# Second mixture-of-experts FFN: one shared-expert block moved behind the expert tiles, with its weights' loads, bias adds and combines rearranged

## The reference, cut to what matters

```
x = x + 0.5 * ffn(layernorm(x));  x = x + attn(layernorm(x));  x = x + 0.5 * ffn(layernorm(x))

ffn(x):                                   # 4096 tokens, D = 256
  weights, idx = gate(x)                  # 2 of 16 experts per token
  h  = silu(x @ We1[e] + be1[e]) * (x @ We3[e] + be3[e])     # 128 wide
  y  = sum over the 2 chosen of weight * (h @ We2[e] + be2[e])
  z  = silu(x @ ws1 + bs1) * (x @ ws3 + bs3) @ ws2 + bs2     # shared, 256 wide
  return y + z
```

## Time and profile before

| | |
|---|---|
| median of 3 runs | 1149.94 us (1148.79 to 1150.99) |
| profiled execution | 1148.11 us, its span 1146.4 us |
| busy share of the span | TensorE 90%, ScalarE 76%, VectorE 67%, GpSimd 40% |
| head (routing, four shared blocks) | about 877 to 929.5 |
| turns | 929.5 to 1093.5 |
| tail (four shared blocks, 16 combines, output) | 1093.5 to 1146.4 |

### The profile page before, as it was taken

How to read it: one execution, slowest core, us unless ns; L and a number is a source line. 1 busy time by engine, 2 the same in 40 slices (tenths; PEclk the granted TensorE clock), 3 DMA queues, 4 the chain that set the end, 5 groups by cost and what they waited for, 6 DMA issues and landing times.

```text
span 1146.4 us, 23653 instructions
## 1 busy us (share of the span) xinstructions
PE 1028.5 (90%) x7546; PEld 558.4 (49%) x7549; DVE 772.9 (67%) x1565; ACT 871.3 (76%) x1251; POOL 461.9 (40%) x671
## 2 busy tenths in 40 slices
PE   8998999989787787989889998989899988999996
PEld 4456999946554122222122222322224568998854
DVE  6898788768996514544255547467768678678866
ACT  4326777746887999999999999999997236777710
POOL 1003666467730424421222223431413345677755
PEclk8999999999999899999999999999999999999998
DMA  8911555445766121020201022120101944566554
GB/s 288 276 57 51 172 166 169 151 132 174 226 195 207 48 71 56 10 62 10 65 10 54 18 70 79 33 71 19 48 1 38 308 147 150 163 188 180 175 177 152
DMA packets 125717, 133.79 MB, mean 117 GB/s; under 512 B 13224, under 2 KB 111888, under 8 KB 125616
## 3 DMA queue, kind: packets, MB, share of 16 engines
q1 hardware_dynamic: 109056, 90.95, 25.0%
q0 software_dynamic: 14448, 39.47, 12.4%
q10 hardware_dynamic: 2112, 2.10, 0.5%
HBM read 80.43 MB, written 52.04 MB: 116 GB/s over the span
## 4 chain that ended last, share of the span: by engine, by line
PE 26%; ACT 26%; issue 15%; DVE 10%; DVEq 1%; POOL 1%; DMA 1%; ACTq 0%; POOLq 0%
ACT wide L2073 23%; PE banks L2445 6%; PE banks L1957 5%; PE banks L2370 4%; PE banks L2457 3%; PE banks L2379 2%; PE banks L1931 2%; DVE x_res L1628 1%; PE banks L2433 1%; PE banks L1453 1%; DVE wide L1677 1%; DVEq L2653 1%; PE banks L1456 1%; PE banks L1971 1%; DVE attn_lines_parts L190 1%
## 5 line engine op out<-in xcount | busy, mean ns | idle before, releaser
L2073 ACT ACTIVATE wide<-banks 128x1536 f32<-128x1536 f32 (+1 forms) x384 | 492.3, 1491 | 4.2 <-PE banks L1931 3.3
L1957 PE MATMUL banks<-wide,attn_attend_v_now 128*32 128x512 f32 (+3 forms) x2560 | 288.7, 542 | 2.4 <-POOL wide L2083 2.4
L2083 POOL TENSOR_SCALAR_AFFINE_SELECT wide<-wide 128x256 f32<-128x256 f32 (+1 forms) x320 | 116.3, 394 | 387.7 <-ACT wide L2073 385.3
L1931 PE MATMUL banks<-attn_attend_q_now,attn_attend_k_now 32*128 32x512 f16 (+3 forms) x1280 | 150.7, 355 | 56.9 <-ACT wide L2073 53.8
L1931 PEld LDWEIGHTS banks<-attn_attend_q_now,attn_attend_k_now 32*128 32x128 f16 x1280 | 38.7, 91 | 292.5 <-ACT wide L2073 248.3
L668 POOL DMA_INDIRECT f_region<-xn_rows,f_token_of x79 | 78.9, 999 | 124.7 <-DVE f_token_of L899 82.7
L2128 DVE COPY sums<-banks 128x512 f32<-128x512 f32 x32 | 22.1, 691 | 134.3 <-PE banks L1957 134.1
L2445 PE MATMUL banks<-f_xnt 128*128 128x128 f32 x752 | 101.4, 278 | 10.1 <-DVE f_more L2671 7.2
L2133 DVE RECIPROCAL below<-below 128x512 f32<-128x512 f32 x32 | 107.3, 3353 | 1.1
L2445 PEld LDWEIGHTS banks<-f_xnt 128*128 128x128 f32 x752 | 91.3, 191 | 15.1 <-ACT f_xnt L2523 8.8
L2553 POOL DMA_INDIRECT last_rows_in<-xn_rows,f_spare x72 | 70.2, 975 | 66.9 <-DVE f_stage L2614 23.6
(11 more groups left out here) (368 smaller groups left out, 1811.5 us busy)
## 6 DMA issues: line engine op xcount, KB each, us to landing
y_half<-f_xnt SPq DMA_DIRECT2D x94, 128.0 KB
y_slots<-wide SPq DMA_DIRECT2D x79, 128.0 KB, 1.7
attn_v<-f_more SPq DMA_DIRECT2D x32, 256.0 KB
attn_attend_v_now<-attn_v SPq DMA_DIRECT2D x32, 256.0 KB, 3.1
x_res<-L_attn_x SPq DMA_DIRECT2D x8, 512.0 KB, 7.4
xn_rows<-f_w_all SPq DMA_DIRECT2D x8, 512.0 KB, 5.4
attn_q<-attn_lines_q_out SPq DMA_DIRECT2D x8, 512.0 KB, 3.4
attn_k<-attn_lines_k_out SPq DMA_DIRECT2D x8, 512.0 KB, 3.9
```

Of the source, the lines that this page charges most:

```text
L1931: last = pe.matmul(score[i % SLOTS][:, j, column:column + columns(u)], k_now[rows, kt * P:(kt + 1) * P], q_now[rows, qc * QW + c0:(qc + 1) ...
L1957: last = pe.matmul(out_bank[qc][rows, c0:QW], v_now[:, kt, rows], probs[:, place, column:column + columns(u)], start=(kt == 0), stop=(u == ...
L2073: act.activation(probs_flat[:, at:at + width_of[i]], score_flat[i % SLOTS][:, 0:width_of[i]], ACT.Exp, scale=SCALE).then_inc(sem.exp_done, 1)
L2083: pool.affine_select(out=part, in_=part, compare_op=ALU.is_ge, fill=0.0, base=0, pattern=[[0, part.shape[1]], [1, P]], channel_multiplier= ...
```

## The change

- `SHARED_FIRST` goes from 4 to 3: block 3 of the shared expert is computed in the tail, with five blocks there. In the head VectorE's `offset` comes before `add_shared(2)`.
- The rings that lay in the space of `xnt` lie in blocks 0 to 2 of it alone; `y_rows` goes to `s.lin`, the fourth place of `w_up` to a tensor of its own.
- SP issues the loads of We2 and be2 (2 MB each) before it waits for the stores; We1 and We3 stay behind.
- GpSimd adds `bs2` to the second half's blocks, after `bring(11)` and before it waits for `prod_ready`; VectorE's four adds are gone.
- Ten combines lie between turns in place of 16. The rows of tiles 10 to 15 are fetched into places of the row ring whose last turn is over (`left_row`), and combined in the tail.
- The tail's order on VectorE is new: combines in groups, and `add_shared(i)` after the combines of block i (`finish`), where it came before them. SP waits for `z_added` as well. The last two parts of the output are one of two tiles.

```diff
-SHARED_FIRST = 4
+SHARED_FIRST = 3
...
+    w_two, gated = ring(2, UP, 0), ring(2, P, 0)
+    rows_t, w_one = ring(2, D, 1), ring(1, UP, 1)
+    w_up = [w_two[:, 0, :], w_two[:, 1, :], w_one[:, 0, :], w_fourth[:]]
+    y_rows = s.lin[:].rearrange("p f n -> p (f n)").rearrange("p (n w) -> p n w", n=ROUND)
...
+    row_left = {place: n for n in range(TURNS) for place in (row_place(n),)}
+    left_rows = sorted((n, place) for place, n in row_left.items() if place < ROWS - ROWS // 4 or place >= ROWS)
+    def left_row(t, k):
+        return left_rows[TOPK * (t - BACK_LATE) + k]
     def back(t, k):
-        return back_first[:, 2 * (t % BACK_FIRST) + k, :] if t < HT else back_second[:, 2 * (t - HT) + k, :]
+        if t >= HT:
+            return back_second[:, 2 * (t - HT) + k, :]
+        if t >= BACK_LATE:
+            return rows_in(left_row(t, k)[0])
+        return back_first[:, 2 * (t % BACK_FIRST) + k, :]
...
     def sync(sp):
         sp.wait_ge(before.exp_done, ends.exps)
         sp.wait_ge(before.pv_done, ends.values)
+        sp.dma_start(w_all[:, :, UP:UP + D], w["We2"]...)
+        sp.dma_start(w_all[:, :, UP + D:], over_partitions(w["be2"], P, E, D))...
         for q in range(2):
             sp.wait_ge(s.stored[q], 16 * (BLOCKS - 2) // 2)
...
-        sp.dma_start(w_all[:, :, UP:UP + D], w["We2"]...)
-        sp.dma_start(w_all[:, :, UP + D:], over_partitions(w["be2"], P, E, D))...
...
             sp.wait_ge(sem.combined, end_tile)
+            sp.wait_ge(sem.z_added, end_tile // 2)
...
         shared_down(1)
-        shared_up(3, (0, 1))
         pe.wait_ge(first.pairs_ready, 2)
         routing.count(pe, bank[7])
-        shared_up(3, (2, 3))
         shared_down(2)
-        shared_down(3)
...
-            if k == 0 and BACK_FIRST <= t < HT:
+            if k == 0 and BACK_FIRST <= t < BACK_LATE:
                 pool.wait_ge(sem.combined, t - BACK_FIRST + 1)
+            elif BACK_LATE <= t < HT:
+                pool.wait_ge(sem.combined, t - BACK_RING + 1)
+                pool.wait_ge(sem.rows_turned, left_row(t, k)[0] + 1)
...
         for n in range(4, 12):
             bring(n)
+        pool.wait_ge(first.staged, BLOCKS)
+        for b in range(HB, BLOCKS):
+            part = x[:, b * BT:(b + 1) * BT, :]
+            pool.tensor_tensor(part, part, s.bs2..., ALU.add).then_inc(first.bs2_added, 1)
         pool.wait_ge(sem.prod_ready, SHARED_FIRST)
...
         routing.keep_counts(dve, 1, bank[7])
-        multiply(3)
+        routing.offset(dve, 1)
         add_shared(2)
-        routing.offset(dve, 1)
-        add_shared(3)
...
-        for b in range(HB, BLOCKS):
-            part = x[:, b * BT:(b + 1) * BT, :]
-            dve.tensor_tensor(part, part, s.bs2..., ALU.add).then_inc(first.bs2_added, 1)
+        def finish(i):
+            dve.wait_ge(sem.combined, (i + 1) * BT)
+            add_shared(i)
         dve.wait_ge(first.bs2_added, BLOCKS)
-        (multiply 4, 5; add 4; combine 16..18; multiply 6; combine 19; add 5; ...)
+        combine_some(BACK_LATE, HT - 1)
+        multiply(3)
+        combine_some(HT - 1, HT + 2)
+        multiply(4)
+        combine_some(HT + 2, HT + 3)
+        finish(3)
+        combine_some(HT + 3, HT + 6)
+        multiply(5)
+        finish(4)
+        combine_some(HT + 6, HT + 10)
+        multiply(6)
+        finish(5)
+        combine_some(HT + 10, HT + 14)
+        multiply(7)
+        finish(6)
+        combine_some(HT + 14, HT + 16)
+        finish(7)
...
-OUT_PARTS = [... (TILES - 4, TILES - 2), (TILES - 2, TILES - 1), (TILES - 1, TILES)]
+OUT_PARTS = [... (TILES - 4, TILES - 2), (TILES - 2, TILES)]
-COMBINE_AT = (61, 64, 67, 70, 73, 76, 79, 82, 84, 85, 87, 88, 90, 92, 93, 95)
+COMBINE_AT = (61, 64, 67, 70, 73, 76, 79, 82, 85, 88)
+BACK_LATE = len(COMBINE_AT)
```

More of the change, by code:

```diff
@@ L2282, in ffn_by_halves @@
     bs = sb("bs", [P, 2 * SHARED // P])
+    w_fourth = sb("w_fourth", [P, UP])
     ws13, ws2, prod_t, bias_rows = s.ws13, s.ws2, s.prod_t, s.bias_rows
@@ L2289, in ffn_by_halves, with ring @@
     back_second = w_all[:].rearrange("p e f -> p (e f)")[:, 0:HT * TOPK * D].rearrange("p (n d) -> p n d", d=D)
[L2290 to L2297, removed]
+    taken = [0, 0]
+    def ring(n, width, c):
+        at = taken[c]
+        taken[c] += n * width
+        assert taken[c] <= SHARED_FIRST * BW
+        return s.xnt[:, c, at:at + n * width].rearrange("p (n w) -> p n w", n=n)
+    w_two, gated = ring(2, UP, 0), ring(2, P, 0)
+    rows_t, w_one = ring(2, D, 1), ring(1, UP, 1)
+    w_up = [w_two[:, 0, :], w_two[:, 1, :], w_one[:, 0, :], w_fourth[:]]
+    y_rows = s.lin[:].rearrange("p f n -> p (f n)").rearrange("p (n w) -> p n w", n=ROUND)
     sem = semaphores(nc, tag, "experts_loaded bias_turned bias_ready xnt_ready "
@@ L2334, in sync @@
         sp.wait_ge(before.pv_done, ends.values)
+        sp.dma_start(w_all[:, :, UP:UP + D], w["We2"].rearrange("e i d -> i e d")).then_inc(sem.experts_loaded, 16)
+        sp.dma_start(w_all[:, :, UP + D:], over_partitions(w["be2"], P, E, D)).then_inc(sem.experts_loaded, 16)
         for q in range(2):
@@ L2341, in sync @@
                          ).then_inc(sem.experts_loaded, 16)
-        sp.dma_start(w_all[:, :, UP:UP + D], w["We2"].rearrange("e i d -> i e d")).then_inc(sem.experts_loaded, 16)
-        sp.dma_start(w_all[:, :, UP + D:], over_partitions(w["be2"], P, E, D)).then_inc(sem.experts_loaded, 16)
         for n in range(TURNS):
@@ L2444, in up @@
                     col_at = (2 * c + f) * INTER
-                    last = pe.matmul(bank[2 + m][:, f * P:(f + 1) * P], w_up[:, at, col_at:col_at + INTER],
+                    last = pe.matmul(bank[2 + m][:, f * P:(f + 1) * P], w_up[at][:, col_at:col_at + INTER],
                                      rows_t[:, m, c * P:(c + 1) * P], start=(c == 0), stop=(c == DC - 1))
@@ L2573, in gpsimd @@
             bring(n)
+        pool.wait_ge(first.staged, BLOCKS)
+        for b in range(HB, BLOCKS):
+            part = x[:, b * BT:(b + 1) * BT, :]
+            pool.tensor_tensor(part, part, s.bs2.rearrange("p (o d) -> p o d", o=1).to_broadcast([P, BT, D]), ALU.add).then_inc(first.bs2_added, 1)
         pool.wait_ge(sem.prod_ready, SHARED_FIRST)
@@ L2670, in multiply_rows @@
                 dve.wait_ge(sem.y_done, n - ROUND + 1)
-            dve.scalar_tensor_tensor(prod_t[:, at, :], bank[2 + n % 2][:, P:2 * P], w_up[:, at, UP - 1:UP], gated[:, n % 2, :], ALU.add, ALU.mult
+            dve.scalar_tensor_tensor(prod_t[:, at, :], bank[2 + n % 2][:, P:2 * P], w_up[at][:, UP - 1:UP], gated[:, n % 2, :], ALU.add, ALU.mult
                                      ).then_inc(sem.prod_done, 1)
@@ L2675, in combine @@
             dve.wait_ge(fetch_of(t), fetches(t))
[L2676 removed]
+            if t < SHARED_FIRST * BT:
+                dve.wait_ge(sem.z_added, 2 * (t // BT) + t % BT // 2 + 1)
             dve.scalar_tensor_tensor(tile(t), back(t, 0), core.weight[:, 0, t:t + 1], tile(t), ALU.mult, ALU.add).then_inc(sem.first_added, 1)
@@ L2709, in vector, with combine_some @@
                 combine(combine_at[n])
-        for b in range(HB, BLOCKS):
-            part = x[:, b * BT:(b + 1) * BT, :]
-            dve.tensor_tensor(part, part, s.bs2.rearrange("p (o d) -> p o d", o=1).to_broadcast([P, BT, D]), ALU.add).then_inc(first.bs2_added, 1)
-        dve.wait_ge(first.bs2_added, BLOCKS)
[L2714 to L2731, removed]
+        def combine_some(first_tile, end_tile):
+            for t in range(first_tile, end_tile):
+                combine(t)
+        def finish(i):
+            dve.wait_ge(sem.combined, (i + 1) * BT)
+            add_shared(i)
+        dve.wait_ge(first.bs2_added, BLOCKS)
+        combine_some(BACK_LATE, HT - 1)
[15 more added lines that the diff above has]
+        finish(7)
     return Programs(sync, tensor, scalar, gpsimd, vector, (sem, row_loaded, row_stored))
 INVERT_AT, BACK_FIRST, BACK_RING = 26, 4, 2 * BT
-OUT_PARTS = [(t, t + 4) for t in range(0, TILES - 4, 4)] + [(TILES - 4, TILES - 2), (TILES - 2, TILES - 1), (TILES - 1, TILES)]
+OUT_PARTS = [(t, t + 4) for t in range(0, TILES - 4, 4)] + [(TILES - 4, TILES - 2), (TILES - 2, TILES)]
 BACK_TURN = HALF_TURNS + ROWS + LENT + 6
-COMBINE_AT = (61, 64, 67, 70, 73, 76, 79, 82, 84, 85, 87, 88, 90, 92, 93, 95)
+COMBINE_AT = (61, 64, 67, 70, 73, 76, 79, 82, 85, 88)
+BACK_LATE = len(COMBINE_AT)
 FFN_NAMES = "gate_w gate_b We1 be1 We2 be2 We3 be3 ws1 bs1 ws2 bs2 ws3 bs3"
```

4 lines of the change are left out of this document (2 added, 2 removed).

## The result

The changed kernel takes 1154.88 us (median of 5, 1152.8 to 1157.8) against 1150.23 us for the kernel before, measured beside it: ratio 1.0042, 95% interval 1.0029 to 1.0056. It is slower by 4.7 us. The forecast was slower by 2.3 us, 1152.2, with a range up to 1154.8: the measured time lies just outside. The side and the kind of the likeliest case were right; its size was half of what came. In the profiled executions the span went from 1146.4 to 1151.1 us.

A forecast was written before the change was run, and what follows sets the result against it. VectorE was taken to bound the start, its combines the turns' end, the fetches the tail. Start +1.9, turns' end -4.0 and tail +4.4 gave +2.3 us, thus 1152.2 us, range 1145.3 to 1154.8.

The forecast's parts named there:

- the likeliest case: Port held: GpSimd's bias adds keep VectorE's two-SBUF-input operations waiting in the head; 1150.3 to 1154 us, chance 0.60.
- What bounds the start: Start of the tile turns: VectorE binds; one shared block fewer brings the first weights from 932.23 to 927.7, -4.6 us.
- The hold: Routing table in the head: each GpSimd bias add holds one two-SBUF-input VectorE operation for its whole length, +6.5 us.
- so the gap of 0.91 at 912.21 is absorbed: Head: VectorE's 7.4 us lateness uses up its old 0.91 us wait for TensorE's up products, leaving +6.5 us.
- the row of 3.96: Earlier profile: six GpSimd affine_selects, normally 2.15 us, took 3.96 beside a VectorE operation with two SBUF inputs.
- Weights sooner: Head: loading We2 and be2 earlier gains nothing; delayed stores could cost 1.7 us at most, taken as 0.
- Combines moved, -4.0: End of the turns: fewer combines there save 2.5 us, and the stretch to the first shared product shrinks from 3.8 to 2.3.
- Tail, +4.4: Tail: five blocks keep TensorE busy 51.8 us without waits, ending at t + 57.3 against t + 52.9, 4.4 us longer.
- All turns behind them keep their pattern and move along: Tile turns after the first weights: they only shift with the start, with no change in length.
- port free: Rival in the head: GpSimd's adds cost VectorE 0.3 us or nothing; 1145.8 us, chance 0.22.
- the tail out of step: Rival in the tail: late fetches hold VectorE's in-order combines and so TensorE, +2 to +3 us, 1155; chance 0.09.
- the partial hold: Rival in the head: for example only two of four adds meet a two-input operation, +3 us, about 1149; chance 0.09.

The follow-up runs named there:

- a1r: The changed kernel with the four bias adds back on VectorE at the head of the tail; 1146.99 us, ratio 0.9984 to the kernel before.
- c1: The changed kernel with the four bias adds on VectorE directly behind `multiply(0)` and the We2 and be2 loads behind the stores again; 1146.4 us, ratio 0.9969.
- b1r: The kernel before with only the second half's bias adds moved to GpSimd after `bring(11)`; 1155.48 us, ratio 1.0055.
- a3r: The changed kernel with the loads of We2 and be2 back behind the stores; 1154.06 us, ratio 1.0034 to the kernel before.
- a4: The changed kernel with GpSimd's four adds each behind one of `bring(8)` to `bring(11)`, a fetch between each two; 1148.64 us, ratio 0.9994.
- d5: c1 with all 16 first-half combines between the turns again, none of them in the tail; 1150.97 us, ratio 1.0005 to the kernel before.
- a2r: The changed kernel with the four adds still on GpSimd, but after `bring(5)` in place of `bring(11)`; 1147.82 us, ratio 0.9974.
- d6: c1 with block 3 back in the head, four shared blocks ahead and four behind, tail combines regrouped; 1146.75 us, ratio 0.9966.

## Why the prediction was right or wrong

**What bounds the start: right.** VectorE's chain sets the first weights. Without a hold they were to come at 927.7; a1r has 927.50, c1 927.57.

**The hold: right in kind, too small by 1.2 us.** This is the first term that failed, "+6.5 us on VectorE's chain", which measured 7.7. I let VectorE slip in one operation after each add; it got none in until the last was over. That alone changes little, 7.2 against 7.4 us. The step that failed is "so the gap of 0.91 at 912.21 is absorbed". It took the up products at their length of before, 3.60 us, and they took 6.59, since TensorE came out of its own 4.5 us wait at a granted clock of 0.56; so the gap grew to 1.37. b1r and a3r have the same wait of 4.52 us, then 6.60 and 6.44 us for the products, and gaps of 1.37 and 1.22; a1r, without the hold, has 0.90.

The Trainium skill (SBUF — State Buffer, section Who interferes with whom) has the rule that whichever of the two issues first keeps the port for its whole instruction, and the other waits. On the length a4's L1075 agrees: it ends 0.24 us after the third add. On the order it does not show it: by the trace L1075 began 0.36 us ahead of that add and waited all the same, though GpSimd's times in a trace are rough. And by the rule L1072 would have waited for the first add alone, to about 902.5; it was held to 909.75. That VectorE loses its turn between adds that follow directly is thus in addition to the rule, and the measurement decides. Of the two bounds, 0.3 and the whole length, the row of 3.96 pointed to the right one.

**Weights sooner, worth nothing: borne out**, by a3r and by the 11 us that ScalarE leaves them lying. The store of the staged blocks did land later (9.5 us after its issue against 3.6), inside idle time.

**Combines moved, -4.0: right**, -3.84 in the traces and 3.75 in d5 against c1. In part that is luck: index 84 to 93 took 14.0 us (1077.50 to 1091.51) for the forecast 14.4, and from there to the first shared product 2.9 for 2.3.

**Tail, +4.4: nearly right**, +3.84. TensorE's 51.8 us and the change of the limiting engine came as written; the last store with 256 KB took 4.2 us to the end of the span, not 4.8.

**The turns: a term that I had at 0 came out at +1.6.** This is the second step that failed, "All turns behind them keep their pattern and move along", for which I gave no reason. From the first weights to the up product of index 84 the kernel before took 140.57 us and the changed one 142.15. About half of it, 0.8 us, are the two longer stops of VectorE shown above, 0.36 us over turns 4 to 6 and 0.42 over turns 15 to 18. They stand at the same turns in all five traces whose VectorE program has four compute instructions less ahead of the turns than the kernel before (changed, a1r, a2r, a3r, a4), and in none of the five others (before, b1r, c1, d5, d6); c1 and d5 have block 3 in the tail too, but four adds in the head. So these 0.8 us come with the changed program, though not with the block's place, and why VectorE stops there is open. The other half is no cost of the change that these runs could show: from index 6 to index 84 the time is 129.1 us before and 130.3 after; b1r has 128.9, a3r 129.1, d6 129.9, c1 128.8 and d5 130.4. c1 and d5 issue the same work up to the late combines and differ by 1.6, most of it before turn 72, at a granted clock of 1.00 in both. What moves it was not found. As a profiled execution stands for one draw of it, it belonged into the range.

The sum: 3.1 at the start, 1.6 in the turns, -3.8 at their end, 3.8 in the tail, 4.7 us. Forecast were 1.9, 0, -4.0 and 4.4. So the hold's 1.2 and the turns' 1.6 are what was missing, and a tail 0.6 shorter than forecast hid some of it. **The rivals:** port free fell with the first row above, and a2r and a1r show about what it would have been, 1147.8 and 1147.0 (forecast 1145.8); the tail out of step and the partial hold did not come, though a4 makes the latter: 1148.64, forecast about 1149.

## What to carry to other kernels

Work moved from VectorE to GpSimd cost nothing here where VectorE did nothing with two SBUF operands meanwhile, and 5.7 us where it did. Look in the trace for VectorE's operand kinds in the stretch, not for GpSimd's idle time. Here 6.8 us of VectorE's own idle time lay just ahead of the table and took the same four adds at no cost that the time shows, though they held one GpSimd fetch for 3.3 us. A block moved from ahead of the turns to behind them gained only what the engine that binds the start was given, and cost what the tail's limit had no room for: 4.5 against 3.8 us. And a term put at 0 for "the rest moves along" needs a row too: here it was 1.6 us.

## What the runs showed of the hardware

VectorE's operation with two SBUF operands waited through four GpSimd adds in a row, 7.67 us, and through one only (2.96 us) where an indirect DMA stood between the adds. Operations with one SBUF and one PSUM operand ran beside the same adds at their usual length (1.41 and 1.28 us). The other way round, four VectorE adds in a row held one indirect DMA of GpSimd, 4.28 us in place of 0.95, in three kernels. After a wait of 4.5 us TensorE's granted clock was 0.56 over the next 6.7 us, and eight products of 512 columns took 6.59 us in place of 3.60; two other kernels with the same wait had 6.60 and 6.44. One chip of those used ran the kernel before 7% slower, 1230.68 us.
